# First layer of a graph layer kernel: one group of column sums a block, bias rows and normalise on ScalarE, and a new order of a step

## What is computed

```python
def _layer(h, M, W_in, b_in, W_out, b_out, W_self, b_self, gamma, beta):
    A = M / (jnp.sum(M, axis=0, keepdims=True) + EPS)
    mask = A > THRESH
    W = jnp.where(mask, A, 0.0)
    T = h @ W_in + b_in
    weighted_sum = jnp.einsum('ji,jd->id', W, T)
    weight_sum = jnp.sum(W, axis=0)
    has_edge = jnp.any(mask, axis=0)
    agg = jnp.where(has_edge[:, None], weighted_sum / (weight_sum[:, None] + EPS), T)
    agg = agg @ W_out + b_out
    out = agg + (h @ W_self + b_self)
    mu = jnp.mean(out, axis=-1, keepdims=True)
    var = jnp.mean(jnp.square(out - mu), axis=-1, keepdims=True)
    return (out - mu) * jax.lax.rsqrt(var + LN_EPS) * gamma + beta
h = relu(_layer(layernorm(x), adj, ...1)); h = relu(_layer(h, adj, ...2)); x = x + h
```

## Time and profile before

| | |
|---|---|
| median of 3 runs | 1154.63 us (1154.5 to 1156.99) |
| profiled execution | 1147.88 us, span 1146.2 us |
| TensorE, mean granted clock | 0.962 |
| TensorE busy | 1018.1 us, 89% |
| VectorE busy | 608.6 us, 53% |
| ScalarE, POOL busy | 296.3 and 304.0 us |
| first layer | about 50 to 390 us |
| second layer | 390 to about 660 us |

### The profile page before, as it was taken

How to read it: one execution, slowest core, us unless ns; L and a number is a source line. 1 busy time by engine, 2 the same in 40 slices (tenths; PEclk the granted TensorE clock), 3 DMA queues, 4 the chain that set the end, 5 groups by cost and what they waited for, 6 DMA issues and landing times.

```text
span 1146.2 us, 13041 instructions
## 1 busy us (share of the span) xinstructions
PE 1018.1 (89%) x3612; PEld 537.9 (47%) x3612; DVE 608.6 (53%) x1609; ACT 296.3 (26%) x578; POOL 304.0 (27%) x302
## 2 busy tenths in 40 slices
PE   0598999999999999999999289948999999999996
PEld 0344545545545554444444158823454444444443
DVE  6867788787772323344443428863433433433462
ACT  4543534344310000000000034505123123122122
POOL 4703253443443311212222215543110110110110
PEclk9889999999999999999999689978999999999998
DMA  9849654544500068888882563225654654645200
GB/s 359 327 181 360 237 190 177 221 175 192 221 1 1 9 240 319 312 318 309 316 317 87 223 206 111 87 81 193 248 199 178 230 188 189 230 175 202 83 10 10
DMA packets 45357, 220.97 MB, mean 193 GB/s; under 512 B 6626, under 2 KB 27940, under 8 KB 33634
## 3 DMA queue, kind: packets, MB, share of 16 engines
q1 hardware_dynamic: 42144, 215.60, 50.2%
q0 software_dynamic: 2864, 4.39, 1.1%
q10 hardware_dynamic: 274, 0.13, 0.0%
HBM read 210.68 MB, written 11.62 MB: 194 GB/s over the span
## 4 chain that ended last, share of the span: by engine, by line
PE 60%; DVE 20%; issue 6%; DVEq 4%; ACT 4%; ACTq 2%; POOL 2%; DMA 2%; SPq 1%; POOLq 0%
PE PA L1405 26%; PE PA L1591 15%; DVE R L852 12%; PE O L1567 3%; PE O L1634 3%; ACT U L616 2%; ACTq L656 2%; PE T L1654 1%; PE SR L1634 1%; PE O L1613 1%; ACT U L659 1%; PE O L1444 1%; PE PA L1557 1%; DVEq L1282 1%; PE T L1643 1%
## 5 line engine op out<-in xcount | busy, mean ns | idle before, releaser
L1591 PE MATMUL PA<-ring,S 128*128 128x512 f32 x512 | 236.5, 602 | 3.8 <-ACT S L634 2.9
L1405 PE MATMUL PA<-ring,S 128*128 128x512 f32 x512 | 232.2, 603 | 0.0
L1405 PE MATMUL PA<-ring,U 128*128 128x512 f32 x512 | 225.5, 594 | 0.0
L852 DVE TENSOR_TENSOR R<-R,ring 128x1024 f32<-128x1024 f32 x112 | 157.3, 1404 | 16.0 <-issue 9.5
L554 ACT ACTIVATE work<-ring 128x2048 int8<-128x2048 f32 x64 | 122.3, 1910 | 106.4 <-DMA ring<-in_adj_cols 91.0
L1405 PEld LDWEIGHTS PA<-ring,S 128*128 128x128 f32 x512 | 96.5, 193 | 104.9 <-issue 104.0
L1405 PEld LDWEIGHTS PA<-ring,U 128*128 128x128 f32 x512 | 94.9, 190 | 106.8 <-issue 106.7
L1591 PEld LDWEIGHTS PA<-ring,S 128*128 128x128 f32 x512 | 93.2, 193 | 104.9 <-issue 99.4
L1283 DVE TENSOR_TENSOR U<-ring,work 128x512 f32<-128x512 f32 x112 | 82.2, 737 | 91.8 <-PE SR L1634 45.7
L800 POOL DMA_DIRECT2D out_x<-work x7 | 5.9, 844 | 240.0 <-DVE work L1350 240.0
L768 POOL DMA_INDIRECT disp_d<-work x32 | 32.2, 1007 | 122.7 <-DVE work L1154 115.4
(11 more groups left out here) (232 smaller groups left out, 1194.7 us busy)
## 6 DMA issues: line engine op xcount, KB each, us to landing
ring<-in_adj_cols SPq DMA_DIRECT2D x56, 2048.0 KB, 7.4
ring<-in_adjT_cols SPq DMA_DIRECT2D x32, 2048.0 KB, 7.4
ring<-in_Wr SPq DMA_DIRECT2D x1, 4096.0 KB, 12.1
ring<-in_Wr SPq DMA_DIRECT2D x2, 2048.0 KB, 13.6
work<-in_w SPq DMA_DIRECT2D x16, 256.0 KB
disp_d<-U SPq DMA_DIRECT2D x4, 650.0 KB, 12.9
work<-disp_d SPq DMA_DIRECT2D x8, 325.0 KB, 3.2
S<-in_x SPq DMA_DIRECT2D x4, 512.0 KB, 8.9
```

What stands on the lines that cost most here:

```text
L852: nc.vector.tensor_tensor(acc, first if q == 0 and c == 1 else acc, piece, ALU.add)
L1405: mm = nc.tensor.matmul(out_T[:, :], X[:, t * D:(t + 1) * D], ring[slot][t // HT][:, (t % HT) * BW:(t % HT + 1) * BW], start=n == 0, stop= ...
L1591: mm = nc.tensor.matmul(PA[slot][:, :], S[:, t * D:(t + 1) * D], ring[1][t // HT][:, (t % HT) * BW:(t % HT + 1) * BW], start=t == 0, stop= ...
```

## The change

It rewrites the first layer's steps.

1. One group of sums for each block. `sums` after the mask and its semaphore go; sums of a block that was masked are made by VectorE inside the branch (`masked_sums`, much longer code in the branch, still branched over). `ms` holds the sums as a copy in SBUF.
2. The threshold row is written inside the branch only. The row of empty columns comes from ScalarE (`empty_cols`, Relu with scale -1024 and bias 1 from bank SR).
3. Bias rows: ScalarE multiplies (`bias_rows`, four activations of 128 x 256 straight into `z1`), POOL adds the bias in one instruction of 128 x 1024 (`add_bias`).
4. Normalise: VectorE keeps the moments and makes the negated mean, POOL makes the inverse root and the product of both, ScalarE applies them (`normalise`, four Identity activations).
5. The transposes of h read x directly; POOL's copy of it goes, and hT has two buffers.
6. New order on VectorE, TensorE, ScalarE and POOL. SP stores the threshold row after quarter 3 and no longer holds quarters 2 and 3 of block 1 for the first one. The zeros of the fill lie in `U` now, and ScalarE waits for the fills at block 4's step.

```diff
 TensorE
-            def step(k, slot, rnd, has):
+            L1_PIECES = ((2, lambda k: turn_h(k)),
+                         (3, lambda k: k > 0 and out_rows(k - 1, (0, 1))),
+                         (8, lambda k: k > 0 and out_rows(k - 1, (2, 3))),
+                         (18, lambda k: k + 1 < NB and raw_sums(k + 1)),
+                         (20, lambda k: k > 0 and turn_z(k - 1)),
+                         (22, lambda k: k + 1 < NB and sum_verdict(k + 1)),
+                         (24, lambda k: k > 0 and layer2_products(k - 1)))
+
+            def step(k):
                 pe.wait_ge(s_clean, k + 1)
-                sums(BT, s_ms)
-                pe.wait_ge(s_aT, k + 1)
...
+                if k >= 2:
+                    pe.wait_ge(s_aT, k - 1)
+                done = 0
+                for n, piece in L1_PIECES:
+                    products(S, k % 2, done, n, s_quart)
+                    piece(k)
+                    done = n
+                products(S, k % 2, done, NT, s_quart).then_inc(s_agg, 1)
 VectorE
+            def step(k):
+                if k > 0:
+                    collect(k - 1)
+                if k + 1 < NB:
+                    add_quarter(k + 1, 2)
+                if k > 0:
+                    out_tiles(k - 1, (0, 1))
+                if k + 1 < NB:
+                    add_quarter(k + 1, 3, (0, 1))
+                if k > 0:
+                    out_tiles(k - 1, (2, 3))
+                    moments(k - 1)
+                if k + 1 < NB:
+                    add_quarter(k + 1, 3, (2, 3))
+                    fold(k + 1)
+                if k + 2 < NB:
+                    add_quarter(k + 2, 0, (0, 1, 2))
+                if k + 1 < NB:
+                    verdict(k + 1)
+                if k + 2 < NB:
+                    add_quarter(k + 2, 0, (3,))
+                if k + 1 < NB:
+                    mask_if_needed(k + 1)
+                    scales(k + 1)
+                if k > 0:
                     layer2_inputs(k - 1)
+                if k + 2 < NB:
+                    add_quarter(k + 2, 1)
 ScalarE
+            def normalise(k):
+                act.wait_ge(s_rstd, k + 1)
+                alone(act)
+                for t in range(BT):
+                    zt = z1[:, t * DH:(t + 1) * DH]
+                    last = nc.scalar.activation(zt, zt, ACT.Identity, bias=nm[:, t:t + 1], scale=rstd[:, t:t + 1])
+                last.then_inc(s_z, 1)
...
+            for k in range(NB):
                 evac_hT(k)
+                if k + 1 < NB:
+                    check(k + 1, 3)
+                if k > 0:
+                    normalise(k - 1)
+                if k + 1 < NB:
+                    empty_cols(k + 1)
+                if k > 0:
+                    relu_h1(k - 1)
+                bias_rows(k)
+                if k + 2 < NB:
+                    for q in range(3):
+                        check(k + 2, q)
 POOL
+            for k in range(NB):
+                empty_rows(k)
+                if k > 0:
+                    moments(k - 1)
+                add_bias(k)
+                if k > 0:
+                    own_T2(k - 1)
 SP
+            store_thr(0)
+            refill(2)
...
+            store_thr(1)
             for k in range(3, NB):
-                refill(k, k % 2)
+                refill(k)
+                store_thr(k - 1)
```

More of the change, by code:

```diff
@@ L118, in build @@
         sumc, rs_, ws_, rw_, nn = [small[:, 4 * i:4 * i + 4] for i in range(5)]
+        ms, nm = [small[:, 64 + 4 * i:68 + 4 * i] for i in range(2)]
         rbp, cc = [[small[:, 72 + 8 * i + 4 * j:76 + 8 * i + 4 * j] for i in range(2)] for j in range(2)]
@@ L130, in part @@
             return work[:, at:at + n]
-        pA, thr, aT, hT, hs = [part(BW * i, BW) for i in range(5)]
-        pre = [part(5 * BW + DH * i, DH) for i in range(2)]
+        pA, thr, aT = [part(BW * i, BW) for i in range(3)]
+        hT = [part(BW * i, BW) for i in (3, 4)]
+        own = part(5 * BW, BW)
         z1 = part(6 * BW, BT * DH)
@@ L367, in peeled, with blk, cols_of @@
             drain(NB)
[L369 to L375, removed]
+        def blk(k):
             return (NB - 1) - k
+        def cols_of(k):
+            return slice(blk(k) * BW, (blk(k) + 1) * BW)
         ticks = {nc.sync: sem("tick_sp"), nc.scalar: sem("tick_act"), nc.gpsimd: sem("tick_pool"), nc.vector: sem("tick_dve")}
@@ L575, in relu_h1 @@
                 last.then_inc(s_h1T, 1)
[L577 to L591 removed]
+            act.wait_ge(s_const, 1)
+            for q in range(4):
+                check(0, q)
+            empty_cols(0)
+            for q in range(3):
+                check(1, q)
+            act.wait_ge(s_wts, 16 * len(WEIGHTS))
+            act.wait_ge(s_wready, 1)
+            act.wait_ge(s_hn, 2)
+            for k in range(NB):
+                evac_hT(k)
+                if k + 1 < NB:
[8 more added lines that the diff above has]
+                if k + 2 < NB:
+                    for q in range(3):
+                        check(k + 2, q)
+            normalise(NB - 1)
+            relu_h1(NB - 1)
             def step2(k, slot, rnd, prev, nxt):
@@ L979, in collect @@
             def collect(k):
[L981 removed]
+                dve.wait_ge(s_agg, k + 1)
                 alone(dve)
[L983 removed]
+                dve.wait_ge(s_neh, k + 1)
                 alone(dve)
[L986 to L1013 removed]
@@ L1033, in _ @@
             nc.vector.tensor_copy(b_us[:, 0:D], O[1][:, 2 * D:3 * D]).then_inc(s_wready, 1)
-            thresholds(0)
-            verdict(0, 0)
-            mask_if_needed(0, 0)
-            for q in range(3):
-                add_quarter(1, 0, q)
-            peeled1(dve, step)
-            layer2_inputs(NB - 1)
-            collect(NB)
-            nc.vector.tensor_tensor(aT, PA[1][:, :], U[:, 0:BW], ALU.add).then_inc(s_aT, 1)
-            out_tiles(NB, 1, range(BT))
-            normalise(NB)
-            layer2_inputs(NB)
+            verdict(0)
+            mask_if_needed(0)
+            scales(0)
+            for q in range(2):
+                add_quarter(1, q)
+            for k in range(NB):
+                step(k)
+            collect(NB - 1)
+            out_tiles(NB - 1, range(BT))
+            moments(NB - 1)
+            layer2_inputs(NB - 1)
             dve.wait_ge(s_own, NB)
```

392 lines of the change are left out of this document (169 added, 223 removed).

## The result

The changed kernel takes 1139.31 us in the median of 4 runs (1137.47 to 1141.56), the kernel before 1155.81 us (1154.5 to 1157.59) beside it: a ratio of 0.9854 [0.983, 0.9878], 16.5 us faster. The forecast was 1122, 32.6 us under the 1154.63 known then. So the sign was right and the size forecast about double.

What follows compares the result with a forecast made beforehand. A ring of TensorE and VectorE was taken to bound the first layer. Gains of 4.4 (start), 1.2 (step 1) and 5 x (43.2 - 37.9) make 32.1 us: 1115.8 profiled, 1122 as median, range 1112 to 1140.

Steps and rivals of the forecast that it cites:

- VectorE's own work: VectorE's first-layer step: 43.3 us less removed work, waits and shorter adds gives 36.3, including 0.5 of flag wait.
- That makes 37.5, as good as TensorE's 37.8: First-layer step: VectorE's 36.3 us plus 1.0 to 1.3 waiting at layer2_inputs, set beside TensorE's unbroken stream.
- 0.1 us of gaps: TensorE's gaps in a first-layer step after the change, bounds 0 and 3, giving a period of 37.9 us.
- a ring: First-layer step before: TensorE waits for VectorE three times, VectorE for TensorE once and POOL once; the change shortens both.
- Nothing to spare at the fold: VectorE's fold in a steady step ends at 19.5 us; TensorE wants it after product 18 at 19.4.
- contention: VectorE's adds beside POOL: a step over 39.5 us would mean this, seen in their mean, expected about 1.4.
- The start: Steps 0 and 1: 4.4 us gained before step 1's products, then step 1 at 44.6 against 45.8, 1.2 gained.
- The three things that the working took off: VectorE ahead of block 1's fold in step 0: two 512-wide rows and a 0.45 us transfer wait; fold at 71.1, not 73.1.
- B: Rival: VectorE stays behind; POOL contention or a late fold costs 1.5 to 4 us a step, 1131 to 1145; chance 0.24.
- C: Rival: fills end before VectorE needs the quarter (5.0 + 1.7 back) or contention nearly vanishes, 1112 to 1116; chance 0.12.
- E: Rival: POOL's 4.1 us addition and three 512-wide instructions hold VectorE's adds fully; step 45.7 us, total 1162; chance 0.05.
- The sentence that the trace agrees only in part: On the exclusive port lock: adds beside POOL lengthen from 1.23 to 1.77 us, but lose far less than POOL is busy.

Runs made afterwards that it cites:

- e_flag: Changed kernel with the flag sent after product 20 instead of 22, ahead of the transposes of z: 1128.23 us, ratio 0.9849 to the kernel before.
- the scales out of PSUM: Changed kernel with scales reading the sums from their PSUM bank instead of the SBUF copy: 1127.69 us, ratio 0.9837 to the kernel before.
- The cut ring: Changed kernel with the flag after product 20 and two of quarter 1's four adds ahead of the layer-2 inputs: 1135.3 us, ratio 0.9797.
- The kernel with the fills later: Flag after product 20, quarter 1's adds split around layer-2 inputs, and zero fills moved behind quarter 1 of blocks 3 and 4: 1124.71 us, ratio 0.9707.
- b_third: The kernel before, unchanged, on a third chip: 1156.98 us, ratio 1.0006.

## Why the forecast was half right

**Right.** TensorE's work: 38.3 us a step (191.30 in five), and 37.76 unbroken, against 37.8 to 38.5 taken. VectorE's own work: in e_flag, where the flag is not waited for, 39.11 less the waits of 1.80 and 0.97 is 36.3; the forecast's 36.3 had 0.5 of flag wait in it, so 35.8, and 0.3 of the difference is the wait behind the branch: 1.39, against 1.12 in the one step that was read; the step after it in the kernel before has 1.54. The adds: mean 1.394 us in the changed kernel, forecast about 1.4, 1.470 before. Over 15 adds that is 2.5 us above undisturbed ones, 2.1 in the working. No gap before the transposes of z, no table load in the steps, and ScalarE's four normalised tiles and its checks keep nobody waiting. The last step: 35.7 us from its product 0, 35.9 before. A wait for the transfer in step 1 alone.

**The step that failed.** "That makes 37.5, as good as TensorE's 37.8", and then 0.1 us of gaps. The working compared two engines' sums and took the larger. But the prediction's own first part calls this a ring, and a ring is not governed by the larger sum: VectorE's waits for TensorE's outputs and TensorE's waits for VectorE's fold lie on the same path, and add. From VectorE's side the 39.8 of the changed kernel is 36.3 of own work, 1.65 for the flag and 1.9 for the hold. The working had 35.8, 0.5 for the flag, nothing for the hold and 1.2 for the layer-2 outputs: 37.5. So two terms of that column were too small, the flag wait by 1.15 and the hold, put at nothing, by 1.9; with these, the own work (36.3 for 35.8) and the layer-2 wait (none) put right the column gives the 39.8. But it would have misled about what they cost: the scales out of PSUM and the flag moved ahead show that a removed wait comes back as the next one, 3.4 us removed for 0.5 gained. So the form of the sum was wrong as well. The cut ring tests it directly: with no work taken from either engine, the steps fell by 1.2 against the changed kernel and 0.8 against the one with the flag moved. "Nothing to spare at the fold" was in the text; a fold without slack should have been priced as a ring, by following one round (sums to layer-2 outputs, 12.1; layer-2 inputs to fold, 27.0), not as 0.1 of gaps. The prediction named contention as the reading of a step over 39.5, to be seen in the mean of the adds; that mean fell as forecast and the step was 39.8 all the same: the hold falls on small instructions, which that mean does not contain, and the rest is the ring.

In the accounts, five steps are 9.5 of the 12.6 us that were lost at layer 2's begin (371.04 against 358.4), with 39.8 against 37.9 each.

**The start, mis-sized.** Step 1: 46.6 against 44.6. The mechanism was right; VectorE's timeline of the changed kernel in step 1:

```profile
116.02 1.22 DVE L873 TENSOR_TENSOR R<-ring 128x1024 f32<-128x1024 f32 x1 [7.17 <-DMA ring<-in_adj_cols]
```

And TensorE's:

```profile
121.65 0.19 PE L1427 MATMUL SM<-ones,small 128*1 128x1 f32 x2 [6.36 <-DVE small L907]
121.77 3.78 PE L1434 MATMUL PA<-ring,S 128*128 128x512 f32 x4
125.34 4.29 PE L1477 MATMUL O<-W_us,work 128*128 128x256 f32 x16
```

The transfer landed at 116.0 instead of 114.8, because the step before it ended 1.2 late; one of the additions behind it took 3.2 us; so TensorE waited 6.36 instead of 5.0. Behind the gap two products (four passes) took 3.78 where a steady step has 1.98, and the layer-2 products 4.29 where it has 3.62: 2.5 us instead of 1.7. 6.4 + 2.5 are, within 0.1, the 8.8 by which this step exceeds 37.8. The kernel with the fills later shows the term whole: against the cut ring alone, 47.3 - 37.8 = 9.5 us are what the fills ahead of block 3's quarters cost. Step 0: 1.2 late, as the fold came at 72.3 against 71.1. VectorE's rows name most of it: four adds took 5.93 us (60.02) where the four before them took 5.13, and POOL's 128x512 multiplication ran from 59.28 to 60.97; and the wait behind the branch there was 1.71 where it had been 1.39. The three things that the working took off also add up to 1.65 us (0.6, 0.6 and 0.45) and not to the 2.0 between 73.1 and 71.1. The sum 1.2 + 2.0 + 9.5 = 12.7 accounts for the loss.

**The rivals.** What came is B in time (1131 to 1145, a chance of 0.24), by 1.9 us a step, and in part in mechanism: contention with POOL is there, as the hold, and the fold is late by 0.74, but what decided is the round of hand-overs. C's first half (the fills) is real and worth 9.5 us once they are moved, which this change does not do. E did not come: POOL's wide addition ran beside the small instructions and cost VectorE 1.9 us a step, not 4.1, and the three 512-wide ones lengthened a run of four adds from 5.13 (54.70, ahead of POOL's instruction of 59.28) to 6.02 and 6.70 us (218.43 and 250.62), 0.8 to 0.9 each and not 2.06. The sentence that the trace agrees only in part with the Trainium skill's rule ("SBUF — State Buffer", the same section) has to be taken back. In the kernel with the fills later two adds beside POOL's wide addition took 4.53 us instead of 2.53, 2.0 more, and a 512-wide instruction costs somewhat under half of that for half as many elements: that fits an exclusive lock. POOL's recorded length is not the hold: the wide addition is recorded with 2.37 us where it comes first and 2.84 where an add was already running (233.11), so the 2.06 very likely holds a wait of its own. It was E's price that was wrong, by reading POOL's recorded length as its hold.

**The median.** 6.7 us were put between the profiled execution and the median, as an offset. The two new profiles of the kernel before point to what it is: the time between experts, 9.7 us in one and 10.8 to 11.8 in the other, the same code, 10 us apart in the whole kernel (1146.7 and 1156.98). On one chip both kernels had the quick one, on two chips every kernel looked at had the slow one; the profiled execution of before had the quick one, that of the changed kernel the slow one, which is why the profiles differ by only 10.4 us (1147.88 to 1137.47) where layer 2 begins 19.5 earlier. In the slow rhythm ScalarE's first piece comes 2.98 us after the start of the products that it reads (700.05 to 703.03 in b_third), in the quick one 0.74 (690.92 to 691.66 in before's profile), and VectorE's first pieces of an expert are late in the same way. What causes it stays open: no run here changes it. It is also not the whole of what is given back behind the first layer: where both kernels had the quick rhythm, layer 2 began 22.0 us earlier (393.25 and 371.29) and the time fell by 18.8. Those 3 us were not traced. Of the 17.3 us between the forecast and the median, 12.6 are lost before layer 2; the other 4.7 lie behind it and are explained only as far as this.

## What to carry to other kernels

Where two engines hand work to each other several times a step, price the step by following one round of the hand-overs; use the busier engine's sum only if no round is longer. A wait taken away on the round comes back as the next wait until independent work is moved into it; so look for work that can be moved into the wait before taking work off an engine. And before a transfer is blamed or excused, look at what stands ahead of it in its queue: bulk fills whose results are needed hundreds of us later belong behind the first loads.

## What the runs showed of the hardware

VectorE instructions of 128x4 elements took 1.5 to 2.0 us instead of 0.15 beside POOL's 128x1024 addition, until that ended: a tensor_tensor with two SBUF inputs (L970) and tensor_scalar from SBUF to SBUF (L964, L969). A reciprocal from SBUF (0.18) and the three instructions with an input from PSUM (0.13 to 0.16) ran through. POOL's small instructions for the inverse root (1.10 and 1.91 us) did not lengthen the adds beside them: two took 2.53 us at 233.71, as two did at 226.83 with POOL idle. The granted clock fell with a TensorE gap of 4.18 us, to 0.62 in the mean of 13 us behind it; in the changed kernel's steady steps, with gaps of 0.7 to 1.1 us, it stayed at 1.00 (the window 138.05:337.07).
